# A graph attention and mixture-of-experts kernel: four weight matrices prepared each where it is first needed, small loads waited for singly

## What is computed

```python
q = (x @ Wq.T).reshape(B, N, 12, 32)
k = (x @ Wk.T).reshape(B, N, 12, 32)
v = (x @ Wv.T + bv).reshape(B, N, 12, 32)
a = einsum('bnhd,bmhd->bhnm', q, k) * 384 ** -0.5 + adj[:, None]
a = nan_to_num(softmax(where(all(a == 0, -1), -inf, a)))
o = einsum('bhnm,bmhd->bnhd', a, v).reshape(B, N, 384)
x = x_in + o @ Wo.T + bo              # x above is layernorm(x_in)
...
pooled = layernorm(x).mean(axis=1)    # router: top 2 of 4 experts, softmax gates
out = sum over both experts of gate * (act_e(u @ w1[e] + b1[e]) @ w2[e] + b2[e])
x = x + layernorm_with_gain(out + u)  # u = layernorm(x); act is gelu, silu, mish, gelu
```

## Time and profile before

| | |
|---|---|
| median of 3 runs | 1682.14 us (1681.82 to 1683.52) |
| profiled execution, own time | 1679.88 us |
| its span | 1678.1 us |
| TensorE busy with matmuls | 1598.1 us, 95% |
| VectorE, ScalarE, GpSimd busy | 71%, 57%, 49% |
| mean granted TensorE clock | 0.982 |

### The profile page before, as it was taken

The page is one execution under the profiler, slowest core; times in us unless marked ns, Lnnn a source line. Parts: engine busy times, 40 slices in busy tenths (PEclk is TensorE's granted clock), DMA queues, the critical chain, the costliest instruction groups (busy, mean ns, idle before and its releaser), DMA issues.

```text
span 1678.1 us, 44889 instructions
## 1 busy us (share of the span) xinstructions
PE 1598.1 (95%) x12732; PEld 1531.1 (91%) x12733; DVE 1191.3 (71%) x3613; ACT 953.4 (57%) x2780; POOL 826.9 (49%) x1239
## 2 busy tenths in 40 slices
PE   6999999999999999837999999999999999999997
PEld 6899999999999999727999999999999999999997
DVE  4788888888888887776666665666776766567764
ACT  4888888888888888744332332332433423243332
POOL 2777777777777777760233333323333233323333
PEclk9999999999999999958999999999999999999999
DMA  7233333333333332550122222222222222221221
GB/s 242 67 116 114 120 121 121 116 116 121 121 121 121 121 119 97 178 216 20 62 72 70 70 70 70 70 70 70 70 70 70 70 70 70 70 70 62 79 64 36
DMA packets 81260, 159.32 MB, mean 95 GB/s; under 512 B 8672, under 2 KB 46560, under 8 KB 80992
## 3 DMA queue, kind: packets, MB, share of 16 engines
q1 hardware_dynamic: 81120, 157.58, 27.6%
HBM read 94.64 MB, written 62.91 MB: 94 GB/s over the span
## 4 chain that ended last, share of the span: by engine, by line
PE 88%; DVE 5%; ACT 2%; issue 2%; SPq 1%; POOL 1%; DMA 1%; DVEq 0%; POOLq 0%; ACTq 0%
PE bank L368 68%; PE bank L437 5%; PE bank L526 5%; PE bank L396 3%; PE bank L460 3%; PE bank L477 2%; PE bank L469 1%; PE bank L446 1%; DMA x_in<-in_x 1%; DVE half_t L1027 1%; DVE inverse L1034 1%; DVE inverse L1030 1%; ACT at_hi L688 1%; ACT inverse L721 1%; ACT prob L599 1%
## 5 line engine op out<-in xcount | busy, mean ns | idle before, releaser
L368 PE MATMUL bank<-w_hi,ut_in 128*128 x1536 | 423.2, 343 | 32.3 <-issue 27.9
L599 ACT ACTIVATE prob<-att,neg_max 128x128 f32<-128x128 f32 x768 | 297.4, 391 | 34.4 <-DVE neg_max L871 34.3
L368 PEld LDWEIGHTS bank<-w_hi,ut_in 128*128 128x128 f32 x1536 | 280.8, 189 | 37.0 <-issue 37.0
L987 DVE SCALAR_TENSOR_TENSOR at_lo<-bank,gate_col,at_hi 128x384 fp32r<-128x384 f32 x256 | 146.1, 613 | 185.2 <-ACT at_hi L688 185.2
L368 PE MATMUL bank<-w_hi,at_hi 128*128 x768 | 258.0, 336 | 5.6 <-DVE at_lo L987 5.6
L368 PE MATMUL bank<-w_lo,ut_in 128*128 x768 | 257.9, 336 | 0.0
L368 PE MATMUL bank<-w_hi,at_lo 128*128 x768 | 257.1, 335 | 0.0
L368 PE MATMUL bank<-w_lo,at_hi 128*128 x768 | 256.7, 334 | 0.0
L688 ACT ACTIVATE at_hi<-bank,gate_col 128x384 fp32r<-128x384 f32 x256 | 134.5, 576 | 202.9 <-PE bank L526 201.0
L845 POOL TENSOR_SCALAR rs_z<-mv_z 128x1 f32<-128x1 f32 x64 | 14.7, 229 | 473.8 <-DVE mv_z L1053 473.8
L712 ACT ACTIVATE hid<-hid 128x384 f32<-128x384 f32 x192 | 95.1, 527 | 268.9 <-DVE hid L999 268.9
(11 more groups left out here) (136 smaller groups left out, 3820.9 us busy)
## 6 DMA issues: line engine op xcount, KB each, us to landing
xu_scratch<-xu SPq DMA_DIRECT2D x64, 384.0 KB, 2.3
ut_scratch<-ut_out SPq DMA_DIRECT2D x64, 384.0 KB, 2.7
ut_in<-ut_scratch SPq DMA_DIRECT2D x64, 384.0 KB, 2.9
xz<-xu_scratch SPq DMA_DIRECT2D x64, 384.0 KB, 3.0
x_in<-in_x SPq DMA_DIRECT2D x32, 384.0 KB, 4.4
xu<-in_x SPq DMA_DIRECT2D x32, 384.0 KB, 3.5
out_dram<-xz SPq DMA_DIRECT2D x64, 192.0 KB, 1.9
w_lo<-in_L_ffn_w SPq DMA_DIRECT2D x8, 1152.0 KB, 9.8
```

The lines of the kernel that those rows point to most:

```text
L368: last = nc.tensor.matmul(acc, lhs[c][a], rhs[c][b], start=start and n == 0, stop=stop and n == len(terms) - 1)
L599: nc.scalar.activation(prob[g][:, hh, :], att[g][:, head, :], ACT.Exp, bias=neg_max[g][:, head:head + 1], scale=-1.0, accum_out=row_sum[g] ...
L987: nc.vector.scalar_tensor_tensor(out=flat(at_lo[:, s * DC:(s + 1) * DC, :]), in0=at_ps[s][:, 0:HALF], scalar=gate_col[:, col, 1:2], in1=fl ...
```

## The change

On TensorE, ScalarE and VectorE the work on the twelve pieces is taken apart into one group for each matrix, and the groups are put into the steps. Wq is prepared first; TensorE transposes Wk and Wv in step -4 and Wo in step -2; VectorE and ScalarE do their part of Wk and Wv in step -3 and of Wo in step -2. TensorE waits for three pieces before q, six before k, nine before v, and twelve before the scores of graph 0. The load of `bv` gets its own semaphore, waited for at the first `take_v`; the other five small loads are waited for in step 2 on VectorE. On SyncE the input of graphs 2 and 3 moves ahead of Wv, `bv` ahead of Wo, and `bo` behind the first adjacency and residual loads. No arithmetic is added or removed.

```diff
             load_x(0)
-            for m, w in enumerate((Wq, Wk, Wv, Wo)):
-                sp.dma_start(w_raw[m][:], w.rearrange("(c p) d -> p c d", p=P)).then_inc(w_loaded[m], 16)
+            load_projection(0)
+            load_projection(1)
             load_x(1)
-            sp.dma_start(bv_wide[:], ...).then_inc(small_loaded, 16)
-            sp.dma_start(bo_wide[:], ...).then_inc(small_loaded, 16)
+            load_projection(2)
+            sp.dma_start(bv_wide[:], ...).then_inc(bv_loaded, 16)
+            load_projection(3)
             for t in range(2):
                 load_adj(t)
                 load_residual(t)
+            sp.dma_start(bo_wide[:], ...).then_inc(small_loaded, 16)
@@ tensor @@
+            pe.wait_ge(ident_ready, 2)
+            transpose_weights(0)
             for h in STEPS:
-                if h == -2:
+                if h == 0:
                     pe.wait_ge(wt_lo_done, 4 * DC)
...
                 if has(h + 5):
                     transpose_x(h + 5)
+                if h == -4:
+                    transpose_weights(1)
+                    transpose_weights(2)
+                if h == -2:
+                    transpose_weights(3)
@@ scalar @@
+                if h == -3:
+                    round_weights(1)
...
                 if has(h + 5):
                     normalise_x(h + 5)
+                if h == -5:
+                    round_weights(0)
+                if h == -3:
+                    round_weights(2)
+                if h == -2:
+                    round_weights(3)
@@ vector @@
             def take_v(n):
+                if n == 0:
+                    dve.wait_ge(bv_loaded, 16)
...
                 if h == -4:
-                    for n in range(4 * DC):
-                        ...
-                    dve.wait_ge(small_loaded, 16 * (3 + DC))
+                    rest_of_weights(0)
                 if h == 2:
+                    dve.wait_ge(small_loaded, 16 * (2 + DC))
...
                 if has(h + 4):
                     rest_of_x(h + 4)
+                if h == -3:
+                    rest_of_weights(1)
+                    rest_of_weights(2)
...
                 if has(h + 6):
                     input_stats(h + 6)
+                if h == -2:
+                    rest_of_weights(3)
```

More of the change, by code:

```diff
@@ L155, in gnn_moe_kernel @@
         const_ready, small_loaded, ident_ready = sem("const_ready"), sem("small_loaded"), sem("ident_ready")
+        bv_loaded = sem("bv_loaded")
         w_loaded = [sem(f"w_loaded{m}") for m in range(4)]
@@ L264, in load_adj, with load_projection @@
                 sp.dma_start(adj_in[t % 2][:], adj[2 * t:2 * t + 2].rearrange("g n d -> n g d")).then_inc(adj_loaded[t % 2], 16)
+            def load_projection(m):
+                w = (Wq, Wk, Wv, Wo)[m]
+                sp.dma_start(w_raw[m][:], w.rearrange("(c p) d -> p c d", p=P)).then_inc(w_loaded[m], 16)
             load_x(0)
-            for m, w in enumerate((Wq, Wk, Wv, Wo)):
-                sp.dma_start(w_raw[m][:], w.rearrange("(c p) d -> p c d", p=P)).then_inc(w_loaded[m], 16)
+            load_projection(0)
+            load_projection(1)
             load_x(1)
-            sp.dma_start(bv_wide[:], bv.rearrange("(o d) -> o d", o=1).partition_broadcast(P)).then_inc(small_loaded, 16)
-            sp.dma_start(bo_wide[:], bo.rearrange("(o d) -> o d", o=1).partition_broadcast(P)).then_inc(small_loaded, 16)
+            load_projection(2)
+            sp.dma_start(bv_wide[:], bv.rearrange("(o d) -> o d", o=1).partition_broadcast(P)).then_inc(bv_loaded, 16)
+            load_projection(3)
             for t in range(2):
@@ L274, in _ @@
                 load_residual(t)
+            sp.dma_start(bo_wide[:], bo.rearrange("(o d) -> o d", o=1).partition_broadcast(P)).then_inc(small_loaded, 16)
             sp.dma_start(rb_wide[:], router_b.rearrange("(o d) -> o d", o=1).partition_broadcast(P)).then_inc(small_loaded, 16)
@@ L370, in split_product, with transpose_weights @@
                 return last
-            pe.wait_ge(ident_ready, 2)
-            for m in range(4):
+            def transpose_weights(m):
                 pe.wait_ge(w_loaded[m], 16)
@@ L402, in project_qk @@
                 m, t = h % 2, pair(h + 2)
+                if h < 0:
+                    pe.wait_ge(wt_lo_done, (m + 1) * DC)
                 reached(pe, xt_lo_done, 2 * t + 2)
@@ L415, in project_v @@
                 p, cols = slot(n), slice((n % 2) * N, (n % 2 + 1) * N)
+                if n == 0:
+                    pe.wait_ge(wt_lo_done, 3 * DC)
                 reached(pe, xt_lo_done, n + 1)
@@ L573, in _, with round_weights @@
         def _(act):
-            for n in range(4 * DC):
-                act.wait_ge(wt_mm, n + 1)
-                nc.scalar.activation(wt_hi[n // DC][:, n % DC, :], bank[n % 4][:, 0:D], ACT.Copy).then_inc(wt_hi_done, 1)
+            def round_weights(m):
+                for n in range(m * DC, (m + 1) * DC):
+                    act.wait_ge(wt_mm, n + 1)
+                    nc.scalar.activation(wt_hi[m][:, n % DC, :], bank[n % 4][:, 0:D], ACT.Copy).then_inc(wt_hi_done, 1)
             def round_o(n):
@@ L826, in _ @@
                 if h == 0:
-                    pool.wait_ge(small_loaded, 16 * (3 + DC))
+                    pool.wait_ge(small_loaded, 16 * (2 + DC))
                 if has(h - 1):
@@ L858, in _, with rest_of_weights @@
         def _(dve):
+            def rest_of_weights(m):
+                for n in range(m * DC, (m + 1) * DC):
+                    dve.wait_ge(wt_hi_done, n + 1)
+                    nc.vector.tensor_tensor(wt_lo[m][:, n % DC, :], bank[n % 4][:, 0:D],
+                                            wt_hi[m][:, n % DC, :].bitcast(F32), ALU.subtract).then_inc(wt_lo_done, 1)
             def add_bias_and_max(n, quadrants):
```

## The result

| | before | changed |
|---|---|---|
| median of 20 runs each | 1682.11 us (1680.47 to 1683.94) | 1684.58 us (1682.87 to 1686.50) |
| ratio, 95% interval | | 1.0016 (1.0009 to 1.0023) |
| profiled execution, own time | 1679.88 us | 1684.17 us |
| its span | 1678.1 us | 1682.4 us |
| mean granted TensorE clock | 0.982 | 0.980 |

The change costs 2.5 us by the medians. That is inside the bound of 0.2% that was drawn for "no change", and the interval, which leaves 1 out, says that it is nevertheless a loss.

The account below looks back on a forecast made before the run. Bound at the start by the x_in transfer for graphs 4 and 5, behind w1. Queue 1.44, clock 1.39 and transposes 0.1 make 2.9 us, added to the median 1682.14 for 1685.0 us; range 1682.2 to 1687.3.

Parts of the forecast that it names:

- within 0.2%: Whole kernel: time changes by less than the 0.2%, or 3.36 us, that a measurement can tell; chance 0.62.
- the cover: Before project_v(1): the wait for x_in of graphs 4 and 5 hides earlier preparation; at most 0.68 us could show.
- the queue on VectorE: Step -2: three Wo subtractions run between graph 4's statistics and take_v of graph 0, delaying project_v(1) by 1.44 us.
- the clock: TensorE, project_v(1): after idling 6 to 8 us its nine products run at half rate, costing 1.39 us.
- the sum: Start of graph 0's scores: 1.44 + 1.39 + 0.1 = 2.9 us later, all counted through to the end.
- the last sign: TensorE: first transposes of probabilities at about 49.7 us in the profile after, or the forecast is wrong.
- The step that costs the whole earlier start at nothing: Preparation: q starts at 15 to 17 us, 6 to 8 us earlier, counted as 0 us.
- the gain: Rival: x_in for graphs 4 and 5 lands early, so earlier q saves about 5 us, giving 1677.1; chance 0.05.
- The transposes: TensorE, three transposes of graph 4 behind project_v(1): partly slow, costing 0.1 us, with zero and 0.38 as ends.
- the rival with the slow spell through the scores: project_v(1), graph 4's transposes and graph 0's scores all at half rate: 4.1 us, so 1686.3; chance 0.33, or more slowdown included.
- The rule on transposes: Skill page: transposes don't engage full clock, so slowness reaches the scores (1686.3); the forecast instead followed a contrary trace row.
- the landing: DMA queue: x_in for graphs 4 and 5 still lands at 31.67 us, half a microsecond either way.

Follow-up runs that it names:

- e6: Kernel before, with the four loads of w1 moved from the start to steps 4 to 7: 1681.02 us against 1681.29 for the kernel before.
- e7: Changed kernel, with the four loads of w1 moved from the start to steps 4 to 7: 1670.95 us, ratio 0.9944 to the kernel before.
- e11: Changed kernel, unedited, run again beside another run on the same chip: 1684.32 us.
- e1: Changed kernel, with VectorE's three subtractions of Wo moved behind take_v of graph 0: 1683.45 us.
- e4: Kernel before, with only VectorE's three Wo subtractions moved to step -2 behind graph 4's statistics, and TensorE's wait split: 1683.35 us.
- e2: Changed kernel, with 60 unread products added on TensorE behind k of the first pair: 1683.01 us.
- e5: Kernel before, with only VectorE's wait for the small loads moved to the first take_v: 1683.63 us, ratio 1.0018.
- e10: Kernel before, unedited, profiled a second time: x_in for graphs 4 and 5 landed at 31.94 us, scores of graph 0 at 35.39; no run time given.
- e12: Changed kernel with the first loads in the old order, run beside the unedited changed kernel: 1684.66 us against 1684.32.
- e8: Changed kernel with the first loads in the old order, first measurement: 1685.94 us over 6 runs.

## Why the prediction was right, step by step

Predicted 1685.0 us, measured 1684.58, within the range of 1682.2 to 1687.3; "within 0.2%" had the larger chance and came true. The mechanism was right: the cover, the queue on VectorE and the clock. That the figure came out so near is in part luck. In the profiles the change costs 4.1 us from the first transposes of probabilities on, where the sum had 2.9, and the medians show 2.5 to 3.0. Of the signs named ahead of time, the scores were due at 38.0 and started at 39.03, and the transposes of probabilities were due at 49.7 and started at 50.88; by the last sign the sum was wrong, though not the mechanism.

**The cover.** The step that costs the whole earlier start at nothing held: e6 and e7 show both halves of it. With w1 out of the way the old order gains nothing measurable and the new one 10.3 us. The price that I gave the gain, about 5 us, was half of what it is. I had estimated q at 15 to 17 us; it started at 13.10 (14.02 in e11), since ScalarE and VectorE worked off the pieces between the graphs with no wait on VectorE longer than 0.5 us from 9 us on (0.74 in e11). The products of q ran at full rate from the start, 0.12 us apart, where before q began at half rate, 0.21 us apart, and lost time to it.

**The pieces of Wo on VectorE.** Predicted 1.44 us; measured 2.07 - 0.70 = 1.37 in the changed kernel, taken back by e1, and put by itself into the old kernel by e4 (1.40 from landing to scores).

**The clock.** Predicted 1.39 for the products, and measured 3.02 - 1.66 = 1.36; e2 takes it back without removing anything. The transposes were mis-sized: 0.1 predicted, 39.03 - 38.26 = 0.77 against 0.42, or 0.35, measured. The 0.1 was less than the prediction's own reading gives: with the clock back 3.4 us after the first product, nearly half of the transposes' time would have been slow. The scores, costed at nothing, started VectorE 1.30 us behind their own start (39.03 to 40.33), against 1.14 (35.12 to 36.26), and in e11, the same kernel again, 1.61 us behind it (39.04 to 40.65). The clock came back 4.2 us after the first slow product in the one and 4.8 in the other. In e1, by its stretches, it was back at about 37.45, 3.2 us after the first product at 34.26 and in time for the transposes (0.51 us to the scores); in e5 only at 39.5, 5.3 us after. So the rival with the slow spell through the scores is not a rival but the far end of the same mechanism, and e5 shows it whole.

**The rule on transposes.** I went by the row that showed transposes raising the clock, and by the medians the forecast came out nearer than the rule's 1686.3. (The 4.1 us of the profiles equal the rule's sum in number only: 0.8 of them are the landing, and the scores paid 0.2 to 0.5 where it had 0.9.) But the spell lasted longer than that reading gave: three transposes did not end it. e1 and e5, with the same work behind the gap, ended it at the first transposes or with the last scores, so these runs don't decide what part the transposes have in it. The page's sentence that transposes don't engage the full clock (the Trainium skill, "TensorE: Matmul & The Clock Gate", "Part 4: PE-mode transpose") does not hold for these fp32 transposes: the earlier trace rows show it, and so does the start of the changed kernel, where TensorE did nothing but transposes until 13.10 and a group of nine went from 2.15 to 1.15 us:

```profile
5.60 2.15 PE L386 MATMUL bank<-ident,w_raw 128*128 128x128 f32 x9 [5.60 <-DMA w_raw<-in_L_gnn_Wq]
...
10.02 1.15 PE L386 MATMUL bank<-ident,w_raw 128*128 128x128 f32 x9
```

**The landing.** I took it as unmoved, with half a microsecond either way. In the profiles it was at 31.67 and 31.94 in the kernel before, and at 32.48 and 32.49 in the changed one. That 0.5 to 0.8 us is a term that my sum doesn't have. The order of loads does not explain it: with the old order in the changed kernel it was later still, 33.62 and 33.33, and in e4 and e5, which keep the old order, 32.47 and 32.84. The transfer was issued no later, at 18.48 in place of 19.01, and took 13.97 us in place of 12.64. The DMA view shows what lay in its way. Besides the data (q1) it lists a queue that loads instructions (q8), and one packet of 16 KB of it falls into this stretch. In the changed kernel that is from 21.9 to 23.1 us, ahead of the landing (packets, MB, share of the 16 DMA engines):

```profile
q1 hardware_dynamic: 154, 0.47, 98.2%
q8 instruction: 1, 0.02, 5.4%
```

In the kernel before there is none from 18 to 30.9 us, and one from 30.9 to 32.1, as the transfer lands:

```profile
q1 hardware_dynamic: 230, 0.33, 77.2%
q8 instruction: 1, 0.02, 5.7%
```

By the widths of its stretches the packet lasts about a microsecond, on one of the 16 DMA engines, and a transfer has landed only when its last packet has.

The landings tell the same. The four loads of w1 land 2.9 to 3.2 us apart, the input of graphs 4 and 5 1.0 behind them, and that of graphs 6 and 7 1.0 behind that. In each of the twelve profiles that have w1 at the start one of these intervals is longer, by 0.6 to 1.5 us, and it is the one that holds the packet, or, in the three where the packet comes as the input of graphs 4 and 5 lands, the one behind it. In those three (the kernel before, e10, e4) the transfer took 12.64 to 12.70 us; in the nine others 13.4 to 14.1. And the packet follows TensorE's stream: it comes 0.3 to 1.8 us ahead of the end of k in every one of them. So k ten microseconds earlier goes with a packet nine microseconds earlier, ahead of the landing, and e5, which only takes a wait away, does the same (29.4 us, 13.78 in place of 12.64, both issued at 19.0).

That the input of graphs 6 and 7 is issued sooner (19.07 in place of 28.27) is not the cause: in e12 it was issued at 22.17 and in e5 at 25.57, and the interval of that moment was 2.9 us in both, the long one being a later one, with the packet. No run moved the packet and nothing else, so this rests on twelve profiles that agree, not on an experiment. The rest of the differences is mostly in when the transfer was issued, from 18.48 us with the change to 19.76 in e4 and 19.87 in e8.

**The sum.** At the scores the profiles have 39.03 - 35.12 = 3.91 us: landing 0.81, queue 1.37, products 1.36, transposes 0.35, and 0.02 of rounding and hand-over. The second pair of profiles has 39.04 - 35.39 = 3.65. What then becomes of it can be followed. In both pairs `take_v` of the last graph is 4.1 us later, so nothing is given back through the 64 graphs of the attention stage. Before, twice (the first profile and e10), and changed, twice (the first and e11):

```profile
692.36 0.55 DVE L938 TENSOR_TENSOR v_sb<-bank,bv_wide 128x384 f32<-128x384 f32 x1
692.61 0.55 DVE L938 TENSOR_TENSOR v_sb<-bank,bv_wide 128x384 f32<-128x384 f32 x1
696.43 0.55 DVE L972 TENSOR_TENSOR v_sb<-bank,bv_wide 128x384 f32<-128x384 f32 x1
696.72 0.55 DVE L972 TENSOR_TENSOR v_sb<-bank,bv_wide 128x384 f32<-128x384 f32 x1
```

From there to the first `hid` of the expert stage (767.1 in the first profile) the fourteen profiles take from 74.7 to 77.1 us, and the kernel before took both 74.75 and 75.86. An execution's own scatter arises there, and it is as large as half of what the change costs. At the end of the program the medians have 2.5 us (20 runs each) and 3.0 beside e11, so 1.1 to 1.6 us less than the attention stage has. Whether the kernel before loses more in that stretch by its nature, or the few profiles don't stand for the medians, stays open. It is this missing microsecond and more that hides the terms that the sum lacks.

## What to carry to other kernels

Before an order of work is improved at the start of a program, find the transfer that the chain of waits goes through there: as long as it lands no sooner, an earlier start only makes the gap ahead of it longer, and what is now queued behind that wait on its engine is paid in full. Loads that are needed last (here w1, for the expert stage) don't belong ahead of one that a waiting engine needs; this edit and the new order were worth nothing apart and 10 us together. And on TensorE a longer gap is not free even where it was idle anyway: behind waits of 3.00 us and more what followed ran at half clock, behind one of 1.59 (e4) it did not. Nor is a transfer's landing unmoved because the data ahead of it are the same: work that runs sooner loads its instructions sooner, too.

## What the runs showed of the hardware

Taking a wait of 4 us away from VectorE made the kernel 2.3 us slower (e5), two thirds of it in the profile through the granted clock and one third through a later landing. Giving TensorE 10.6 us of products that nobody reads brought the scores 1.7 us nearer to the landing (e2), through the granted clock alone; the changed kernel's time fell by 1.0 to 1.5 us with it, which the intervals of the times do not settle by themselves. The 24 small products of the scores, 32 rows each, are hit too: 0.95 us at full rate, 1.63 and 1.67 at half. Behind the end of k the clock fell 2.0 (e8) to 3.4 us (e1) into the gap, and it came back 3.2 (e1) to 5.3 us (e5) after work began, with the same work behind the gap. So the price of one gap varied: 1.35 us for the products and 0.09 for the transposes in e1, 1.36, 0.35 and 0.7 for products, transposes and scores in e5. And one packet of 16 KB that loads instructions, about a microsecond long on one of 16 DMA engines, came with a landing interval that was 0.6 to 1.5 us longer than its neighbours, in each of twelve profiles.
